# Recurrent block with FP4 side branch on one core: pointwise product and down product in fewer matmuls, down product moved ahead, GpSimd's sum moved, weight remainders made on TensorE

## The chip, the cores and the metric

The kernel runs on 1 core of one Trainium2 chip. The metric is device time in microseconds (us) of one execution. The engines are called by the profile's names: PE is TensorE, DVE is VectorE, ACT is ScalarE, POOL is GpSimd, SP is SyncE.

## What is computed

For x of 16 x 512 x 256 (batch, position, feature), with all products in float32 precision:

```python
xn = layernorm(x)
# branch s
a  = pointwise(causal_dwconv3(rmsnorm(xn, g0))) + b + xn       # 256 -> 256, over positions
hg = rmsnorm(a, g1) @ gru_w.T                                   # 256 -> 512, hidden and gate
h  = scan: h[t] = (1-sig(gate))*h[t-1] + sig(gate)*g(hidden)    # along the positions
b2 = h + a
s  = gelu(rmsnorm(b2, g2) @ w1.T + b1) @ w2.T + bias2 + b2      # 256 -> 1024 -> 256
# branch g, operands rounded to FP4 in blocks of 16 with a scale each
g  = silu( fp4(silu(fp4(xn) @ fp4(w_gate).T) * (fp4(xn) @ fp4(w_up).T)) @ fp4(w_down).T )   # 256 -> 704 -> 256
out = x + s * g
```

## The kernel before

**Tiling.** The program handles the batch in 16 chunks c = 0..15, each of L = 512 positions, as T = 4 token tiles of P = 128 (t); features are KD = 2 blocks of 128, the ff width is KF = 8 blocks, and the FP4 branch's 704 is KI = 6 blocks (NFULL = 5 full ones and a LAST of 64). Weights are loaded and prepared once, within chunk 0.

**Precision.** Except for the pointwise product, each operand is a pair of F32R tiles, a high part (`_hi`, an ACT copy) and a remainder (`_lo`, a DVE or POOL subtraction), and `product` (L982 to L991) issues three matmuls: hi.hi, hi.lo, lo.hi. `pointwise` (L1008) multiplies `pw` and `y` in float32. Transposes on PE are float32 matmuls against `ident`.

**Order.** There is no scheduler: each engine runs the program that is written out by hand, `first()`, then `body(c, front)` for c = 1..15, then `tail(15)`. Semaphores tie the engines. A body interleaves three chunks: gate_up, gru and ff1 of chunk c, the FP4 half behind `hid` and ff2 of chunk c-1, and the norm, FP4 rounding, convolution and pointwise of chunk c+1 (`front_...`).

**PE in a body** (L1239): gate_up(c,0,.), hq_transposes(c-1,1), gate_up(c,1,.), sum_squares, down(c-1,1), gate_up(c,2,.), spread_scale, hq_transposes(c-1,2), gate_up(c,3,.), down(c-1,2), gru(c), hq_transposes(c-1,3), ff2(c-1,0), ff2(c-1,1), sum_squares, down(c-1,3), spread_scale, ff2(c-1,3), ff2(c-1,2), ff1(c) with the transposes of `xc` in its middle, hq_transposes(c,0), transposes of `xq`, pointwise(c+1), down(c,0). One gate_up(c,t,u) is 12 matmuls of 352 columns, a `down` is 18 of 256, gru 24 of 512, ff2 for a tile 2 transposes and 24 of 256.

**What `down` waits for.** For each token tile: hidden (L496, DVE) multiplies `sl` (ACT) with the bank of gate_up; DVE rounds it to FP4 (L401 to L427, into `hq`); PE transposes `hq` (L1058); ACT copies the high part (`hqt_hi`, L812); DVE makes `hqt_lo` (L519, `hidden_low`); then `down` may start.

**The rms norms.** DVE adds the squares (`add_squares`, L524), PE transposes them (`sum_squares`), DVE sums and clamps (`clamp_sums`), POOL takes the power -1/2 (`inv_rms`, L348), PE spreads it (`spread_scale`), DVE scales (`scaled`, L539) and makes `xs_lo` (L545) beside ACT's `xs_hi`.

**POOL** also adds the residual for a whole chunk (`output_sum`, L356, 128 x 1024). Its wait `actlo_ready >= KF*(c+1)+5` lets it start when DVE has made five of the next chunk's eight `act_lo` tiles; two last chunks have no such wait. In chunk 0 POOL makes the remainders of the gru, w1 and w2 weights (`low_weights`, L363), while DVE and PE quantise and split the FP4 weights; PE fills gaps with small matmuls (`keep_busy`, L996).

## Time and profile before

| | us |
|---|---|
| three runs | 1084.11, 1086.87, 1087.17 |
| median | 1086.87 |
| the profiled execution | 1085.26 |
| its span, first to last instruction | 1083.5 |
| PE busy | 1061.8 (98%) |
| DVE busy | 934.5 (86%) |
| ACT busy | 607.3 (56%) |
| POOL busy | 147.5 (14%) |

The trace belongs to the profiled execution; 1.8 us of it lie outside the span. A row of the timeline has the start in us from the span's beginning, the length, engine, line, operation, output <- inputs, shapes and count, and, in brackets, how long the engine sat idle before it and what ended that. Neighbouring matmuls overlap in the rows, so the price of one is the distance between starts, not the length. Matmul ends are modelled.

### The profile page before, as it was taken

The page shows a single profiled execution, that of the slowest core. Times are in us where ns is not written, and L with a number is a line of the kernel's source. Part 1 is how long each engine was busy: PE and PEld are TensorE (multiplying, and loading weights), DVE is VectorE, ACT ScalarE, POOL GpSimd, SP SyncE. Part 2 cuts the span into 40 slices and gives each one's busy share as a digit, 9 for nine tenths or more (in the row PEclk, how much of TensorE's full clock was granted, in tenths as well). Part 3 has the DMA queues.
Part 4 walks back from the last instruction along what each step waited for, and adds up shares of the span by engine and source line. Part 5 has one row for each costly group of instructions (what it writes and reads, how often), then busy time and mean ns, then how long its engine had stood idle before and what let it go on. Part 6 is the DMA issues. An engine that isn't in the chain of part 4 may idle for free. (4 is left out here: it accounts for less than half of the span.)

```text
span 1083.5 us, 18319 instructions
## 1 busy us (share of the span) xinstructions
PE 1061.8 (98%) x6954; PEld 967.9 (89%) x6954; DVE 934.5 (86%) x1720; ACT 607.3 (56%) x967; POOL 147.5 (14%) x123
## 2 busy tenths in 40 slices
...
DMA packets 29365, 31.45 MB, mean 29 GB/s; under 512 B 1120, under 2 KB 28512, under 8 KB 29280
## 3 DMA queue, kind: packets, MB, share of 16 engines
...
## 5 line engine op out<-in xcount | busy, mean ns | idle before, releaser
L990 PE MATMUL gu_ps<-gu_hi,xq_hi 128*128 128x352 f32 x512 | 168.3, 329 | 0.0
L990 PE MATMUL gu_ps<-gu_lo,xq_hi 128*128 128x352 f32 x512 | 165.9, 324 | 0.0
L990 PE MATMUL gu_ps<-gu_hi,xq_lo 128*128 128x352 f32 x512 | 165.7, 324 | 0.0
L990 PE MATMUL w_ps<-w_hi,act_hi 128*128 128x256 f32 x480 | 140.1, 292 | 0.0
L990 PE MATMUL w_ps<-w_hi,act_lo 128*128 128x256 f32 x480 | 135.1, 281 | 0.0
L990 PE MATMUL w_ps<-w_lo,act_hi 128*128 128x256 f32 x480 | 134.9, 281 | 0.0
L990 PE MATMUL w_ps<-dn_hi,hqt_hi 128*128 128x256 f32 x384 | 116.6, 304 | 2.0 <-DVE hqt_lo L519 2.0
L990 PE MATMUL w_ps<-dn_hi,hqt_lo 128*128 128x256 f32 x384 | 108.5, 283 | 0.0
L990 PE MATMUL w_ps<-dn_lo,hqt_hi 128*128 128x256 f32 x384 | 108.4, 282 | 0.0
L818 ACT ACTIVATE g<-w_ps 128x256 f32<-128x256 f32 x64 | 24.7, 385 | 147.7 <-PE w_ps L990 147.6
L496 DVE TENSOR_TENSOR hid<-sl,gu_ps 128x704 f32<-128x704 f32 x64 | 56.8, 887 | 58.8 <-PE gu_ps L990 58.2
L990 PE MATMUL gu_ps<-xs_hi,w_hi 128*128 128x512 f32 x256 | 102.5, 400 | 0.4 <-DVE xs_lo L545 0.4
L990 PE MATMUL gu_ps<-xs_lo,w_hi 128*128 128x512 f32 x256 | 101.0, 395 | 0.0
L990 PE MATMUL gu_ps<-xs_hi,w_lo 128*128 128x512 f32 x256 | 101.0, 395 | 0.0
L990 PEld LDWEIGHTS gu_ps<-gu_hi,xq_hi 128*128 128x128 f32 x512 | 96.7, 189 | 0.2 <-issue 0.2
L990 PEld LDWEIGHTS gu_ps<-gu_lo,xq_hi 128*128 128x128 f32 x512 | 96.6, 189 | 0.0
L990 PEld LDWEIGHTS gu_ps<-gu_hi,xq_lo 128*128 128x128 f32 x512 | 96.3, 188 | 0.0
L842 ACT ACTIVATE act<-gu_ps,cols 128x512 f32<-128x512 f32 x128 | 86.1, 687 | 13.7 <-PE gu_ps L990 13.3
L812 ACT CAST hqt_hi<-w_ps 128x768 fp32r<-128x768 f32 x64 | 51.3, 802 | 73.0 <-PE w_ps L1058 72.2
L356 POOL TENSOR_TENSOR o<-o,x_res 128x1024 f32<-128x1024 f32 x15 | 36.1, 2403 | 400.8 <-issue 393.4
L990 PEld LDWEIGHTS w_ps<-w_lo,act_hi 128*128 128x128 f32 x480 | 90.6, 189 | 0.0
L990 PEld LDWEIGHTS w_ps<-w_hi,act_hi 128*128 128x128 f32 x480 | 90.4, 188 | 0.0
...
## 6 DMA issues: line engine op xcount, KB each, us to landing
...
```

The costliest lines, as they stand in the source:

```text
L356: nc.gpsimd.tensor_tensor(o[:], o[:], x_res[:], ALU.add).then_inc(out_ready, 1)
L496: V.tensor_tensor(hid[:, t, :].rearrange("p (h n) -> p h n", h=2), sl[:], gu_ps[:, 1, :, 0:HALF], ALU.mult).then_inc(hid_ready, 1)
L812: A.copy(hqt_hi[:], hqt_ps).then_inc(hqthi_ready, 1)
L818: A.activation(g[:, t, :], bank[:, 0:D], ACT.Silu).then_inc(g_ready, 1)
L842: A.activation(act1[:, j, :], ff1_bank(j), ACT.Gelu, bias=b1c[:, j:j + 1]).then_inc(gelu_ready, 1)
L990: done = M.matmul(psum, l, r, start=first and i == 0, stop=last and i == len(terms) - 1)
```

## The change

- **Pointwise.** `pw` and `y` become F32R pairs (`pw_hi`, `pw_lo`, `y_hi`, `y_lo`). A chunk's four float32 products become twelve F32R ones of 512 columns. ACT makes `y_hi` (2 copies a chunk), DVE `y_lo` (2 subtractions). All eight `xn` transposes stand ahead of the products.
- **Down.** `hq` now holds its last 64 columns twice (a second DVE instruction of 128 x 64), so the half-empty sixth block carries the high part in its lower and the remainder in its upper 64 rows of `hqt_hi`; `hidden_low` becomes two instructions. `down` has 17 matmuls instead of 18.
- **Order in a body, PE.** down(c-1,3) stands ahead of the squares' transposes; the `x2b` transposes of ff2 are split off (`ff2_open`); ff2(c-1,3) stands ahead of spread_scale, and the `xc` transposes ahead of ff2(c-1,2) and ff1.
- **Order in a body, DVE.** From chunk 2 on, bn_stats of chunk c+2 stands at the end of body c, and its aggregation (`front_moments`) in the next body behind hidden_values(c-1,2); the taps stand ahead of the rounding of `xq`; output(c-1,1) and `front_rows` are earlier. gelus_low is cut 4 + 4 instead of 5 + 3.
- **POOL.** The sum waits for 4 instead of 5 `act_lo` tiles, and in the two last chunks for all 8 (before: none). `low_weights` is gone.
- **Chunk 0.** The remainders of gru, w1 and w2 come from PE: ten pieces of 128 x 512, each a float32 matmul ident x source and an F32R one minus_ident x high part, copied by ACT (`weight_remainder`). DVE's and ACT's work in `first()` is re-ordered, and ff1 is interleaved with the FP4 weights; DVE's rounding of FP4 weight pieces 4 and 5 stands behind `scaled_low(1)`.
- **Last chunk.** In `tail`, ff2 of a tile stands ahead of its down, and DVE makes all `act_lo` before it rounds tile 2.
- **SP.** load(i+3) ahead of store(i).

```diff
 with sp.Fori(0, B - 3) as i:
+    load(i + 3)
     store(i)
-    load(i + 3)
 store(B - 3)
 store(B - 2)
 for t in range(T):
...
 def output_sum(c):
     pool.wait_ge(sg_ready, T * (c + 1))
-    if c < B - 2:
-        pool.wait_ge(actlo_ready, KF * (c + 1) + 5)
+    pool.wait_ge(actlo_ready, KF * (c + 1) + (4 if c < B - 2 else KF))
     pool.wait_ge(xres_ready, 16 * (c + 1))
     nc.gpsimd.tensor_tensor(o[:], o[:], x_res[:], ALU.add).then_inc(out_ready, 1)
...
-def front_moments(c):
+def fp4_hidden_values(dst, rounded):
+    n, last = NBI * FP4_BLOCK, NFULL * P // FP4_BLOCK
+    fp4_values(dst[:, 0:n], NBI, rounded)
+    return V.scalar_tensor_tensor(blocks(dst[:, n:KI * P], NBI - last),
+                                  blocks(q_m[:, NFULL * P:n].bitcast(BF16), NBI - last),
+                                  1.0 / UNIT, spread(q_scale[:, last:NBI], NBI - last),
+                                  ALU.mult, ALU.mult)
...
+def front_y_low(c):
+    for k in range(KD):
+        dve.wait_ge(yhi_ready, KD * c + k + 1)
+        V.tensor_tensor(y_lo[:, k, :], y[:, k, :], y_hi[:, k, :].bitcast(F32),
+                        ALU.subtract).then_inc(ylo_ready, 1)
...
-    fp4_values(hq[:, t % 2, 0:NI], NBI, rounded).then_inc(hq_ready, 1)
+    fp4_hidden_values(hq[:, t % 2, :], rounded).then_inc(hq_ready, 1)
...
     dve.wait_ge(hqthi_ready, T * c + t + 1)
     dve.wait_ge(dn_done, T * c + t)
-    V.tensor_tensor(hqt_lo[:], hqt_ps, hqt_hi[:].bitcast(F32), ALU.subtract).then_inc(hqtlo_ready, 1)
+    V.tensor_tensor(hqt_lo[:], hqt_ps[:, 0:NFULL, :], hqt_hi[:, 0:NFULL, :].bitcast(F32), ALU.subtract)
+    twin = hqt_hi[LAST:P, NFULL, :]
+    V.tensor_tensor(twin, hqt_ps[LAST:P, NFULL, :], twin.bitcast(F32),
+                    ALU.subtract).then_inc(hqtlo_ready, 1)
...
     hidden_values(c - 1, 1, fp4_round(NBI, carried["ratios"]))
-    gelus_low(c - 1, range(5))
+    gelus_low(c - 1, range(4))
     hidden(c, 0)
     scales = hidden_scales(c - 1, 2)
...
     clamp_sums(c * 2, w_ps[:, 0, :])
     hidden_values(c - 1, 2, fp4_round(NBI, ratios))
-    gelus_low(c - 1, range(5, KF))
+    if front and c > 1:
+        front_moments(carried["stats"])
+    gelus_low(c - 1, range(4, KF))
     hidden(c, 2)
     scaled(c * 2, x1, w_ps[:, 1, :], (x1_ready, KD * (c + 1)))
     scales = hidden_scales(c - 1, 3)
     dve.wait_ge(dve_step, ratios)
     hidden(c, 3)
     hidden_values(c - 1, 3, fp4_round(NBI, ratios))
-    if front:
-        front_moments(c + 1)
+    if front and c == 1:
+        front_moments(front_stats(c + 1))
     recurrence(c, 0)
     recurrence(c, 1)
     hidden_low(c - 1, 3)
...
         front_rows(c + 1)
+    clamp_sums(c * 2 + 1, gu_ps[:, 0, 0, :])
+    output(c - 1, 1, w_ps[:, 1, :])
     scales = hidden_scales(c, 0)
     scaled(c * 2 + 1, x1, gu_ps[:, 0, 1, :], (x2_ready, KD * (c + 1)))
     scaled_low(c * 2 + 1)
-    output(c - 1, 1, w_ps[:, 1, :])
     ratios = fp4_ratios(hid[:, 0, :], NBI, scales)
     hidden_values(c, 0, fp4_round(NBI, ratios))
     output(c - 1, 3, w_ps[:, 3, :])
     output(c - 1, 2, w_ps[:, 2, :])
     if front:
-        front_fp4_values(c + 1, front_fp4_ratios(c + 1))
+        ratios = front_fp4_ratios(c + 1)
         front_taps(c + 1)
+        front_fp4_values(c + 1, fp4_round(T * NBD, ratios))
+        front_y_low(c + 1)
         carried["ratios"] = fp4_ratios(hid[:, 1, :], NBI, hidden_scales(c, 1))
         hidden_low(c, 0)
         front_fp4_low(c + 1)
+        if c + 2 < B:
...
+def front_y_high(c):
+    for k in range(KD):
+        act.wait_ge(y_ready, KD * c + k + 1)
+        act.wait_ge(pw_done, KD * c)
+        act.wait_ge(x2_ready, KD * c)
+        A.copy(y_hi[:, k, :], y[:, k, :]).then_inc(yhi_ready, 1)
...
     high_part(c * 2 + 1, (hidden_done, KD * (c + 1)))
     biased_residual(c)
-    for j in range(KF // 2):
+    gelus(c, (0,))
+    if front:
+        front_y(c + 1)
+    gelus_high(c, (0,))
+    for j in range(1, KF // 2):
         gelus(c, (j,))
         gelus_high(c, (j,))
     if front:
-        front_y(c + 1)
-        gelus(c, range(KF // 2, KF))
+        gelus(c, range(KF // 2, KF - 2))
+        front_y_high(c + 1)
+        gelus(c, range(KF - 2, KF))
         hq_columns(c, 0)
         front_xq(c + 1)
...
 def pointwise(c):
+    pe.wait_ge(y_ready, KD * (c + 1))
     for e in range(KD):
-        pe.wait_ge(y_ready, KD * (c + 1))
         for t in range(T):
             M.matmul(w_ps[:, e, t * P:(t + 1) * P], xn[:, t, e * P:(e + 1) * P], ident[:],
                      is_transpose=True, start=t == 0, stop=False)
+    pe.wait_ge(yhi_ready, KD * (c + 1))
+    pe.wait_ge(ylo_ready, KD * (c + 1))
+    for e in range(KD):
         for k in range(KD):
-            last = product(w_ps[:, e, :], pw[:, k, e * P:(e + 1) * P], y[:, k, :], False, k == KD - 1)
+            last = product(w_ps[:, e, :], (pw_hi[:, k, e * P:(e + 1) * P], pw_lo[:, k, e * P:(e + 1) * P]),
+                           (y_hi[:, k, :], y_lo[:, k, :]), False, k == KD - 1)
         last.then_inc(pw_done, 1)
...
 def down(c, t, bank=w_ps[:, 2, :]):
     pe.wait_ge(hqthi_ready, T * c + t + 1)
     pe.wait_ge(hqtlo_ready, T * c + t + 1)
-    for k in range(KI):
-        last = product(bank[:, 0:D], (hqt_hi[:, k, :], hqt_lo[:, k, :]),
-                       (dn_hi[:, k, :], dn_lo[:, k, :]), k == 0, k == KI - 1)
-    last.then_inc(dn_done, 1)
+    for k in range(NFULL):
+        product(bank[:, 0:D], (hqt_hi[:, k, :], hqt_lo[:, k, :]), (dn_hi[:, k, :], dn_lo[:, k, :]),
+                k == 0, False)
+    M.matmul(bank[:, 0:D], hqt_hi[:, NFULL, :], dn_lo[:, NFULL, :], start=False, stop=False)
+    M.matmul(bank[:, 0:D], hqt_hi[:, NFULL, :], dn_hi[:, NFULL, :], start=False,
+             stop=True).then_inc(dn_done, 1)
...
+def ff2_open(c, t, bank, free):
+    pe.wait_ge(x2b_ready, KD * (c + 1))
+    pe.wait_ge(*free)
+    tok = slice(t * P, (t + 1) * P)
+    for k in range(KD):
+        M.matmul(bank[:, k * P:(k + 1) * P], x2b[:, k, tok], ident[:], is_transpose=True,
+                 start=k == 0, stop=False)
+def ff2(c, t, bank):
     pe.wait_ge(acthi_ready, KF * (c + 1))
     pe.wait_ge(actlo_ready, KF * (c + 1))
-    pe.wait_ge(x2b_ready, KD * (c + 1))
-    if free:
-        pe.wait_ge(*free)
     tok = slice(t * P, (t + 1) * P)
-    for k in range(KD):
...
+def remainder(i, free):
+    j, k, h = pieces[i]
+    cut = slice(h * L, (h + 1) * L)
+    pe.wait_ge(whi_ready, KD * j + k + 1)
+    pe.wait_ge(minus_ready, 1)
+    if free:
+        pe.wait_ge(*free)
+    M.matmul(piece_bank(i), ident[:], split_weights[j][1][:, k, cut], start=True, stop=False)
+    M.matmul(piece_bank(i), minus_ident, split_weights[j][2][:, k, cut], start=False,
+             stop=True).then_inc(rest_done, 1)
...
     gru(c, 1)
     hq_transposes(c - 1, 3, (g_ready, T * c - 1))
-    ff2(c - 1, 0, w_ps[:, 0, :], (ss_ready, 2 * c + 1))
-    ff2(c - 1, 1, w_ps[:, 1, :], (xs_ready, KD * (2 * c + 1)))
+    ff2_open(c - 1, 0, w_ps[:, 0, :], (ss_ready, 2 * c + 1))
+    ff2_open(c - 1, 1, w_ps[:, 1, :], (xs_ready, KD * (2 * c + 1)))
+    ff2(c - 1, 0, w_ps[:, 0, :])
+    ff2(c - 1, 1, w_ps[:, 1, :])
+    down(c - 1, 3)
     sum_squares(c * 2 + 1, gu_ps[:, 0, 0, :], (coef_ready, KD * c + 1))
-    down(c - 1, 3)
+    ff2_open(c - 1, 3, w_ps[:, 3, :], (hqtlo_ready, T * c))
+    ff2(c - 1, 3, w_ps[:, 3, :])
     spread_scale(c * 2 + 1, gu_ps[:, 0, 1, :], (cand_ready, KD * c + 1))
-    ff2(c - 1, 3, w_ps[:, 3, :], (hqtlo_ready, T * c))
-    ff2(c - 1, 2, w_ps[:, 2, :], (g_ready, T * c))
-    ff1(c, range(KF // 2))
     if front:
         pe.wait_ge(sg_ready, T * c - 2)
         front_xc(c + 1)
+    ff2_open(c - 1, 2, w_ps[:, 2, :], (g_ready, T * c))
+    ff2(c - 1, 2, w_ps[:, 2, :])
+    ff1(c, range(KF // 2))
+    if front:
         ff1(c, range(KF // 2, KF))
         hq_transposes(c, 0, (sg_ready, T * c))
...
+    down(c, 0, w_ps[:, 0, :])
+    hq_transposes(c, 1, (hqtlo_ready, T * c + 1))
+    last_open(0)
+    last_open(1)
+    last_ff2(0)
+    down(c, 1, w_ps[:, 1, :])
+    last_ff2(1)
+    for t in range(2, T):
+        hq_transposes(c, t, (hqtlo_ready, T * c + t))
+        last_open(t)
+        last_ff2(t)
+        pe.wait_ge(g_ready, T * c + t - 1)
         down(c, t, w_ps[:, t % 2, :])
-        if t < T - 1:
-            hq_transposes(c, t + 1, (hqtlo_ready, T * c + t + 1))
-        ff2(c, t, gu_ps[:, t // 2, t % 2, :], None)
 over_chunks(first, body)
```

What stands in a row at three places. **DVE in a body, from the second hidden product (L496 before, L511 now) to the third.** `hid` is the gated product, `hq` its FP4 values, `act_lo` the gelu remainders, `moments` the layernorm's. Before:

```order
L496 TENSOR_TENSOR hid<-sl,gu_ps 128x704
L413 SCALAR_TENSOR_TENSOR q_y<-hid,q_inv 128x704
L529 TENSOR_REDUCE ss_sum<-w_ps 128x4
L531 TENSOR_SCALAR ss_row<-ss_sum 128x4
L421 TENSOR_SCALAR q_e<-q_y 128x704
L423 TENSOR_SCALAR q_e<-q_e 128x704
L427 SCALAR_TENSOR_TENSOR hq<-q_e,q_scale 128x704
L512 TENSOR_TENSOR act_lo<-act,act_hi 128x512 x3
L496 TENSOR_TENSOR hid<-sl,gu_ps 128x704
```

and now:

```order
L548 TENSOR_REDUCE ss_sum<-w_ps 128x4
L550 TENSOR_SCALAR ss_row<-ss_sum 128x4
L419 TENSOR_SCALAR q_e<-q_y 128x704
L421 TENSOR_SCALAR q_e<-q_e 128x704
L425 SCALAR_TENSOR_TENSOR hq<-q_e,q_scale 128x704
L432 SCALAR_TENSOR_TENSOR hq<-q_e,q_scale 128x64
L447 MEMSET carrier 128x1
L449 BN_AGGR moments<-stats 128x2 x4
L453 TENSOR_SCALAR ln_in<-moments 128x4
L455 TENSOR_SCALAR rms_t<-moments 128x4
L527 TENSOR_TENSOR act_lo<-act,act_hi 128x512 x4
L511 TENSOR_TENSOR hid<-sl,gu_ps 128x704
```

The short duplicate, the aggregation and a fourth `act_lo` have come in between.

**PE in a body, around the second squares' transposes (`gu_ps<-ident,xs`).** `act` rows are ff2, `dn`/`hqt` rows are down(c-1,3). Before:

```order
L990 MATMUL w_ps<-w_lo,act_hi 128x256
L990 MATMUL w_ps<-w_hi,act_lo 128x256
L1042 MATMUL gu_ps<-ident,xs 128x128 x4
L990 MATMUL w_ps<-dn_hi,hqt_hi 128x256
L990 MATMUL w_ps<-dn_lo,hqt_hi 128x256
```

and now:

```order
L1063 MATMUL w_ps<-dn_hi,hqt_lo 128x256
L1146 MATMUL w_ps<-dn_lo,hqt_hi 128x256
L1147 MATMUL w_ps<-dn_hi,hqt_hi 128x256
L1119 MATMUL gu_ps<-ident,xs 128x128 x4
L1184 MATMUL w_ps<-ident,x2b 128x128 x2
L1063 MATMUL w_ps<-w_hi,act_hi 128x256
```

The down product has moved ahead of the transposes, ff2's tile 3 follows them, and the last two down rows are the merged sixth block.

**PE at the end of a body, the pointwise product.** `xn` is the residual that is transposed into the bank. Before:

```order
L1002 MATMUL gu_ps<-ident,xq 128x128 x8
L1013 MATMUL w_ps<-ident,xn 128x128 x4
L990 MATMUL w_ps<-cand,pw 128x512 x2
L1013 MATMUL w_ps<-ident,xn 128x128 x4
L990 MATMUL w_ps<-cand,pw 128x512 x2
L990 MATMUL w_ps<-dn_hi,hqt_hi 128x256
```

and now:

```order
L1075 MATMUL gu_ps<-ident,xq 128x128 x8
L1086 MATMUL w_ps<-ident,xn 128x128 x8
L1063 MATMUL w_ps<-y_hi,pw_hi 128x512
L1063 MATMUL w_ps<-y_lo,pw_hi 128x512
L1063 MATMUL w_ps<-y_hi,pw_lo 128x512
```

The transposes stand together, and the triple of F32R rows comes four times.

## Rows read from the trace of the kernel before

**Rows 1.** The page: busy time of each engine, share of the span, instructions.

```profile
PE 1061.8 (98%) x6954; PEld 967.9 (89%) x6954; DVE 934.5 (86%) x1720; ACT 607.3 (56%) x967; POOL 147.5 (14%) x123
```

**Rows 2.** Busy time by stretch; after the engines PEclk, DMA share, GB/s.

```profile
core 0: us, PE busy (x) PEld busy (x) DVE busy (x) ACT busy (x) POOL busy (x), PEclk, DMA share, GB/s
223.00:287.00 64.00, 63.79 (x418) 58.12 (x417) 56.04 (x104) 36.80 (x59) 8.77 (x7) 1.00 0.08 25
102.00:104.00 2.00, 2.00 (x11) 2.00 (x11) 1.83 (x4) 0.37 (x2) 0.00 (x0) 0.50 0.00 0
1058.00:1060.00 2.00, 0.29 (x3) 0.05 (x1) 2.00 (x5) 1.66 (x2) 0.00 (x0) 1.00 0.00 0
```

**Rows 3.** Chain that ended last: start, us, engine, output, line, matmuls.

```profile
994.01 1.72 PE w_ps L990 x4
...
1000.02 3.87 PE gu_ps L990 x24
...
1019.80 2.14 PE w_ps L990 x18
...
1021.94 5.57 PE gu_ps L990 x24
...
1058.29 1.74 issue
```

**Rows 4.** Timeline of PE: start of body 2, and the body from 488 us.

```profile
168.13 0.33 PE L990 MATMUL gu_ps<-gu_hi,xq_hi 128*128 128x352 f32 x1
...
488.03 0.33 PE L990 MATMUL gu_ps<-gu_hi,xq_hi 128*128 128x352 f32 x1
...
507.82 0.28 PE L990 MATMUL w_ps<-dn_hi,hqt_hi 128*128 128x256 f32 x1
...
525.39 0.65 PE L1050 MATMUL gu_ps<-ident,inv_rms 128*128 128x128 f32 x4 [0.22 <-POOL inv_rms L348]
```

**Rows 5.** Timeline of DVE in the same body.

```profile
492.18 0.89 DVE L496 TENSOR_TENSOR hid<-sl,gu_ps 128x704 f32<-128x704 f32 x1 [2.86 <-PE gu_ps L990]
...
496.69 0.89 DVE L496 TENSOR_TENSOR hid<-sl,gu_ps 128x704 f32<-128x704 f32 x1 [0.37 <-PE gu_ps L990]
...
503.13 0.89 DVE L496 TENSOR_TENSOR hid<-sl,gu_ps 128x704 f32<-128x704 f32 x1 [0.34 <-PE gu_ps L990]
...
506.61 0.89 DVE L519 TENSOR_TENSOR hqt_lo<-w_ps,hqt_hi 128x768 fp32r<-128x768 f32 x1
...
513.60 0.18 DVE L444 BATCH_NORM_AGGREGATE moments<-stats 128x2 f32<-128x6 f32 x1
...
514.16 0.68 DVE L551 SCALAR_TENSOR_TENSOR cand<-gu_ps,cand 128x512 f32<-128x512 f32 x1
...
526.82 1.22 DVE L539 TENSOR_TENSOR xs<-gu_ps,x 128x512 f32<-128x512 f32 x2
...
529.28 1.29 DVE L545 TENSOR_TENSOR xs_lo<-xs,xs_hi 128x512 fp32r<-128x512 f32 x2 [1.24 <-ACT xs_hi L799]
...
541.04 0.75 DVE L480 SCALAR_TENSOR_TENSOR cand<-w_ps,cols,cand 128x511 f32<-128x511 f32 x1 [1.01 <-ACT cand L756]
...
550.21 3.09 DVE L512 TENSOR_TENSOR act_lo<-act,act_hi 128x512 fp32r<-128x512 f32 x5
```

**Rows 6.** Timelines of POOL and DVE: residual sum, and DVE instructions beside POOL.

```profile
489.45 2.41 POOL L356 TENSOR_TENSOR o<-o,x_res 128x1024 f32<-128x1024 f32 x1 [28.10 <-issue]
...
1044.20 2.40 POOL L356 TENSOR_TENSOR o<-o,x_res 128x1024 f32<-128x1024 f32 x1 [7.38 <-DVE o L566]
...
1044.95 1.70 DVE L403 TENSOR_SCALAR q_wide<-q_amax 128x44 f32<-128x44 f32 x1
...
38.62 2.46 DVE L413 SCALAR_TENSOR_TENSOR q_y<-hid,q_inv 128x512 f32<-128x512 f32 x1
```

**Rows 7.** Timeline of PE at the end of chunk 0 and start of body 1.

```profile
100.41 0.36 PE L990 MATMUL w_ps<-dn_hi,hqt_hi 128*128 128x256 f32 x1 [1.97 <-DVE hqt_lo L519]
...
103.39 0.49 PE L990 MATMUL gu_ps<-gu_hi,xq_hi 128*128 128x352 f32 x1
```

More of the change, by code:

```diff
@@ L93, in mixed_recurrent_kernel @@
         ident = sb("ident", [P, P])
-        minus_ident = sb("minus_ident", [P, P], F32R)
         neg_half = sb("neg_half", [P, T])
@@ L101, in mixed_recurrent_kernel @@
         b1c = cols[:, KD * 9:KD * 9 + KF]
-        pw = sb("pw", [P, KD, D])
+        pw_hi = sb("pw_hi", [P, KD, D], F32R)
+        pw_lo = sb("pw_lo", [P, KD, D], F32R)
         gru_hi = sb("gru_hi", [P, KD, 2 * D], F32R)
@@ L137, in mixed_recurrent_kernel @@
         xs_lo = sb("xs_lo", [P, KD, L], F32R)
-        keep = sb("keep", [P, KD, L])
+        keep, y_hi = shared_home(("keep", [P, KD, L], F32), ("y_hi", [P, KD, L], F32R))
         take = xs
-        cand = sb("cand", [P, KD, L])
+        cand, y_lo = shared_home(("cand", [P, KD, L], F32), ("y_lo", [P, KD, L], F32R))
         y = cand
@@ L151, in mixed_recurrent_kernel @@
         hqt_hi = sb("hqt_hi", [P, KI, P], F32R)
-        hqt_lo = sb("hqt_lo", [P, KI, P], F32R)
+        hqt_lo = sb("hqt_lo", [P, NFULL, P], F32R)
         q_amax = sb("q_amax", [P, 64])
@@ L253, in mixed_recurrent_kernel, with piece_bank @@
                          (ld_w2, w2_f, halves(w2_hi), halves(w2_lo)))
+        pieces = [(j, k, h) for j, halved in ((0, 1), (1, 2), (2, 2)) for k in range(KD) for h in range(halved)]
+        def piece_bank(i):
+            return w_ps[:, 2 + i, :] if i < KD else w_ps[:, i % 2, :]
         def ff1_bank(j):
```

256 lines of the change are left out of this document (142 added, 114 removed).

## The prediction

> **What bounds the kernel now.** I read the page's busy shares first, then busy time by stretch, the chain that ended last, and the timelines of PE and DVE over one body. The shares name PE: 98% busy, DVE 86%, ACT 56% [rows 1]. By stretch, 64 us in the middle hold 63.79 us of PE and 56.04 us of DVE [rows 2]. Bodies 2 to 14 are alike: the first product of body 2 starts at 168.13 and that of body 15 at 1000.02 [rows 3, 4], so 13 periods of 63.99 us. In one period PE loses only about 0.4 us, before spread_scale, where it waits for POOL's inv_rms (0.22 us by the modelled ends, 0.42 us by the starts) [rows 4]. So PE's own work sets the period. The reader should see two things more: a matmul taken off PE counts in full only as long as DVE stays in time, and DVE has just 8 us of room in 64, spread over many small gaps.
>
> **Prices on PE.** By the chain, 4 instructions of the float32 pointwise take 1.72 us, so the 8 of a chunk (4 products, two instructions each) take 3.44; 24 F32R matmuls of 512 columns take 5.57, 0.232 each; a down of 18 takes 2.14, 0.119 each [rows 3].
>
> **The steady body, PE alone.** Pointwise: 12 x 0.232 = 2.79 instead of 3.44, -0.65. Down: four times one matmul, -0.48. The wait before spread_scale: today the squares' transposes are followed by one down (2.14) and then by 0.42 of waiting, so DVE's clamp and POOL's power need 2.56. In the new order ff2's tile 3 stands there, 24 x 0.119 + two transposes = 3.06, so the wait goes: -0.42, and -0.07 for a small gap ahead of the squares, which down(c-1,3) now covers. Splitting off ff2's transposes moves work and costs nothing, since consecutive starts add up either way. PE's own need falls by 1.62 to 62.37 us.
>
> **The steady body, what DVE adds.** Per chunk: y_lo, two subtractions at 0.60 from start to start, as act_lo of the same shape (five in 3.09 [rows 5]); four duplicates of 128 x 64, bounded by 0.07 (a twelfth of the 0.8 that hidden's 704 columns take) and 0.18 (the small aggregate at 513.60), I take 0.14; hidden_low in two instructions, +0.05 each. About 2 us, so 58 of 62.4. The question is where. Three places have to be followed.
>
> (a) *Tile 2's down.* hidden(c,1) starts when gate_up ends, at 496.69, and DVE's chain from there reaches the end of hqt_lo for down(c-1,2) at 506.61 + 0.89 = 507.50; PE starts that down at 507.82 [rows 4, 5]. Of these 10.81 us, 0.34 are a wait (at 503.13). Now the aggregation of the moments comes into this stretch (from 513.60 to 514.16 it takes 0.56), a fourth act_lo (0.60), a duplicate (0.14), the split (0.05): +1.35. It may use up the 0.34 wait and about 0.2 of the 0.32 margin, the rest being latency, and PE comes 0.12 earlier: PE waits about 0.9 us. hidden_low is needed there, so nothing hides it. From both sides: 0.6 if the duplicate and the split are nothing and the aggregation overlaps, 1.3 if each is twice as long.
>
> (b) *POOL's sum.* Today it starts at 489.45, just as DVE, done with five act_lo, waits for gate_up until 492.18, 2.86 us: nobody is hurt [rows 5, 6]. Where it does meet DVE, in the last body, it starts at 1044.20 and lasts 2.40 to 1046.60, and DVE's q_wide of 44 columns, issued at 1044.95, takes 1.70, where small instructions take 0.2 (0.18 at 513.60): it ends when POOL ends. Beside low_weights an instruction of 512 columns with two SBUF inputs takes 2.46, where that width takes 0.75 (541.04) [rows 5, 6]. Now the fourth act_lo frees the sum. When is that? DVE from scaled(2c+1) at 526.82 to the fifth act_lo at 550.21 + 3.09 = 553.30 takes 26.48, with waits of 1.24 and 1.01 [rows 5]. Without the waits, plus y_low (1.2, and 0.25 for ACT's y_hi), bn_stats (1.4), duplicates and split (0.3), 0.1 for xs_hi, less output(1) (0.33) and one act_lo (0.6): 26.6. PE from spread_scale (525.39) to the next gate_up (488.03 + 63.99) takes 26.6 now, 22.8 after the change (ff2's tile 3 is ahead of it, 3.06, and 0.65 + 0.12 go). DVE begins about 0.7 behind spread_scale's start, so the fourth act_lo ends 4.5 us into the next body, where today hidden(c,0) starts 4.15 in (492.18 against 488.03) [rows 4, 5]. The wait of 2.86 has been filled up, and POOL's sum runs from 4.6 to 7.0, beside hidden, the reduce and q_wide. Hidden and reduce go on, q_wide (due at 6.2) stands until 7.0. From there small instructions, the squares' sum and hidden_low take 2.2, so hqt_lo for down(c-1,1) ends 9.2 in, where PE wants it at 8.8 (two pairs of gate_up at 3.87 [rows 3], and transposes for 1.1): PE waits 0.5. Bounds: 0 (the sum finds a gap) to 1.5 (hidden itself is blocked).
>
> The Trainium skill bears on this, and against the change: its page "SBUF — State Buffer", section "Who interferes with whom", says that DVE and GpSimd share one port pair as an exclusive lock, that a tensor_scalar in a two-port mode or a DVE instruction with two SBUF inputs stands until GpSimd's instruction ends, and that an instruction with one SBUF input does not. By that rule q_wide waits and hidden (one input in PSUM) and the reduce pass, which gives 1076; without such a lock it would be 1069, the first rival. The trace's 1.70 and 2.46 agree with the rule.
>
> (c) *Tile 0's down and ff1.* y_hi, y_lo and the x transposes come about 1 us ahead of the pointwise, xs_lo 1 us ahead of ff1, hqt_lo of tile 0 0.3 us ahead of its down, by the same addition. No wait here, but little room: +0 to 0.5.
>
> A wait in (b) delays hidden(c,1) and so adds to (a). Together 1.4, and 0.1 for refilling PE: the period is 62.37 + 1.5 = 63.85, that is 0.14 less than now, 13 x 0.14 = **1.8 us**. Nearly all of the 1.62 a body that PE saves would turn into waits for DVE.
>
> **Chunk 0.** Today low_weights holds DVE up beside the w1 and the w2 remainders, each time a q_wide and a q_y, by about 1.7 us each (2.46 - 0.75) [rows 5, 6]; two idles of 2 us on PE (one of 1.97 is at 100.41) are each followed by a stretch at the lower clock (0.50 at 102 us) [rows 2, 7]. Against that, the pieces cost PE 10 x (0.86 + 0.23) = 10.9 us, but mostly in place of keep_busy matmuls, and pw_lo, which waits for pw's load, delays xn by about 1 us. Following DVE, ACT and PE through the new order, gru starts as now, the recurrence 3.4 us and ff1 4 us earlier (two of the four hold-ups are ahead of the recurrence), and the first gate_up of body 1 at 98 instead of 103.39 [rows 7]: **5.4 us** less, give or take 3. ACT, which makes ten more copies of 0.65 us, is what could cost most of this.
>
> **Body 1.** It takes 64.74 now, 0.75 over the period, through the low clock; that goes. It has no early aggregation, so (a) is 0.35 and (b) nearly nothing: **2.0 us** less.
>
> **Body 15 and tail.** The body saves as much as it waits. In the tail, PE idles 1.74 us for act_lo [rows 3]; that goes, as DVE makes them first, and the four shorter downs save 0.5; but the last product is now a down, behind which ACT's silu stands (about 0.5 us), and POOL's sum now falls into the tail (0.5): **1.5 us** less.
>
> **Sum.** 5.4 + 2.0 + 1.8 + 1.5 = 10.7. Span 1083.5 - 10.7 = 1072.8; with the 1.8 outside, 1074.6 for an execution that stood at 1085.26. The median of the runs stands 1.6 above that one: 1076.
>
> **Rivals.**
> *One wait only.* If (b) does not occur (the sum slips between), the period is 63.3, a further 13 x 0.55 = 7 us: 1069. For it: the bounds reach 0. Against it: DVE has no gap left there.
> *No new wait.* PE keeps its 62.37: 13 x 1.62 = 21 instead of 1.8: 1057. For it: PE is 98% busy and sets everything today. Against it: the addition in (a) rests on rows in the same places and needs an error of 0.9 us in 11.
> *The start gives nothing, or DVE is 0.5 us later a body:* 5.4 + 3 or 6.5 us are lost, 1083 to 1087: no change.
> *Slower: PE's clock falls at the new waits.* The wait in (a) is behind a full stretch and might be longer than I think. Behind the idle of 1.97 us at 100.41 the granted clock is 0.50, and the 18 matmuls to 103.39 take 2.98 instead of 2.14; with body 1's 0.75 that is 1.6 us for each fall [rows 2, 7]. Thirteen falls cost 21 us: 1097. It decides once a wait reaches about 2 us; an idle of 1.74 in the tail shows a clock of 1.00 [rows 2, 3], and I expect 0.9. The same price comes if hidden is blocked by the sum (1.5 a body).
>
> **How the numbers follow.** Forecast 1076 with 0.45, its own range 1070 to 1082; one wait 0.2; no wait 0.12; no change 0.1; slower 0.13. The range reaches from no new wait, 1057, to the forecast with the start 3 us and each body 0.7 us worse, 1088. A measurement of this kernel tells about 0.3% (3.3 us) from no change: faster 0.77, same 0.1, slower 0.13.
>
> **What would show it.** Right: a period of 63.7 to 64.0; PE idle for hqt_lo twice a body, at tile 1 (0.5) and tile 2 (1.0), and none before inv_rms; q_wide near 1 us long beside POOL's sum, itself 4.6 us into the body; body 1 starting near 98. Wrong: a period near 62.4 with no such waits, or PEclk under 1.00 in the middle.

## The result

| | before | after |
|---|---|---|
| median of the runs | 1086.86 | 1079.26 |
| the runs | 1084.11 to 1087.17 | 1078.19 to 1079.53 |
| the profiled execution | 1085.26 | 1078.19 |
| its span | 1083.5 | 1076.4 |

The changed kernel is 7.6 us faster, a ratio of 0.993 with a 95% interval of 0.991 to 0.995. I had forecast 1076.0, so the direction and nearly the size came true; of the 10.7 us that the sum promised, the span gave 7.1. In parts (starts of bodies 1, 2 and 15, and the end):

| stretch | before | after | gain | forecast |
|---|---|---|---|---|
| chunk 0 | 103.39 | 99.07 | 4.3 | 5.4 |
| body 1 | 64.74 | 63.10 | 1.6 | 2.0 |
| 13 bodies, each | 63.98 | 63.93 | 0.6 in all | 1.8 in all |
| body 15 and tail | 83.64 | 83.10 | 0.5 | 1.5 |

All starts are the first gate_up product of a body on PE's timeline: for before [rows 4, 7] and, for body 15,

```profile
999.86 0.32 PE L990 MATMUL gu_ps<-gu_hi,xq_hi 128*128 128x352 f32 x1
```

(the chain in [rows 3] has 1000.02, since it begins a piece where the matmul ahead of it ends), and for after

```profile
99.07 0.32 PE L1063 MATMUL gu_ps<-gu_hi,xq_hi 128*128 128x352 f32 x1
...
162.17 0.32 PE L1063 MATMUL gu_ps<-gu_hi,xq_hi 128*128 128x352 f32 x1
...
993.30 0.32 PE L1063 MATMUL gu_ps<-gu_hi,xq_hi 128*128 128x352 f32 x1
```

A period below is the mean of these 13 bodies; in the changed kernel a single body is up to 0.1 us off it.

The page of the changed kernel, busy time and share of each engine (before: [rows 1]):

```profile
PE 1046.4 (97%) x6914; PEld 969.0 (90%) x6914; DVE 978.1 (91%) x1883; ACT 626.5 (58%) x1010; POOL 124.2 (12%) x116
```

PE is busy 15.4 us less and the span is 7.1 shorter; DVE is busy 44 us more. The body that I had followed ([rows 4, 5]), now on PE (start, length, what; in brackets the idle time and what ended it); the rows are the body's start, down(c-1,1) and down(c-1,2):

```profile
481.87 0.32 PE L1063 MATMUL gu_ps<-gu_hi,xq_hi 128*128 128x352 f32 x1
...
491.15 0.36 PE L1063 MATMUL w_ps<-dn_hi,hqt_hi 128*128 128x256 f32 x1 [0.29 <-DVE hqt_hi L537]
...
503.05 0.36 PE L1063 MATMUL w_ps<-dn_hi,hqt_hi 128*128 128x256 f32 x1 [0.83 <-DVE hqt_hi L537]
```

and on DVE and POOL:

```profile
486.28 0.88 DVE L511 TENSOR_TENSOR hid<-sl,gu_ps 128x704 f32<-128x704 f32 x1
487.08 0.88 DVE L399 TENSOR_REDUCE q_amax<-hid 128x44 f32<-128x704 f32 x1
487.99 0.97 DVE L401 TENSOR_SCALAR q_wide<-q_amax 128x44 f32<-128x44 f32 x1
...
538.54 1.29 DVE L498 TENSOR_TENSOR y_lo<-cand,y_hi 128x512 fp32r<-128x512 f32 x2 [0.17 <-ACT y_hi L803]
```

```profile
486.50 2.42 POOL L367 TENSOR_TENSOR o<-o,x_res 128x1024 f32<-128x1024 f32 x1 [28.18 <-issue]
```

PE no longer waits for inv_rms; it waits twice a body for `hqt_lo` (whose second instruction writes `hqt_hi`), ahead of down(c-1,1) and down(c-1,2). POOL's sum starts 4.63 us into the body, and q_wide, small as it is, takes 0.97. Three rows of the waits, in the whole trace (engine and output that waited, who was waited for):

```profile
PE w_ps L1063 <- DVE hqt_hi L537: 16.7, 30, 1.1
...
DVE y_lo L498 <- ACT y_hi L803: 2.4, 13, 0.2
...
PE w_ps L1063 <- DVE y_lo L498: 0.8, 1, 0.8
```

The columns are us in total, times, the longest.

### The profile page after: what moved, and what is told of

It is laid out like the page before. It is cut to its first block, busy times and chain, and to the rows that moved or that the text cites. A ratio compares the mean times of both kernels' runs of the same rounds, so it can differ in the third digit from the quotient of the medians.

```text
span 1076.4 us, 18518 instructions
## 1 busy us (share of the span) xinstructions
PE 1046.4 (97%) x6914; PEld 969.0 (90%) x6914; DVE 978.1 (91%) x1883; ACT 626.5 (58%) x1010; POOL 124.2 (12%) x116
## 4 chain that ended last, share of the span: by engine, by line
PE 47%; DVE 36%; issue 8%; ACT 7%; ACTq 0%; DMA 0%; DVEq 0%
PE w_ps L1063 22%; PE gu_ps L1063 17%; DVE act_lo L527 5%; ACT act L888 4%; DVE hid L511 3%; DVE q_amax L399 3%; DVE hqt_lo L534 2%; DVE hq L425 2%; DVE xs L558 2%; DVE q_wide L401 2%; DVE xq_lo L504 2%; DVE y_lo L498 2%; DVE stats L441 2%; DVE q_y L411 1%; PE w_ps L1135 1%
## 5 line engine op out<-in xcount | busy, mean ns | idle before, releaser
L1063 PE MATMUL w_ps<-dn_hi,hqt_hi 128*128 128x256 f32 x320 | 92.9, 290 | 16.7 <-DVE hqt_hi L537 16.7
L1063 PEld LDWEIGHTS w_ps<-w_hi,act_lo 128*128 128x128 f32 x480 | 90.6, 189 | 0.0
L1063 PE MATMUL w_ps<-dn_hi,hqt_lo 128*128 128x256 f32 x320 | 90.3, 282 | 0.0
L1063 PE MATMUL w_ps<-dn_lo,hqt_hi 128*128 128x256 f32 x320 | 90.0, 281 | 0.0
L360 POOL TENSOR_TENSOR inv_rms<-ss_row,neg_half 128x4 f32<-128x4 f32 x32 | 35.9, 1120 | 456.6 <-DVE ss_row L550 456.6
```

Of the source, the lines that this page charges most:

```text
L360: nc.gpsimd.tensor_tensor(inv_rms[:], ss_row[:], neg_half[:], ALU.pow).then_inc(inv_ready, 1)
L1063: done = M.matmul(psum, l, r, start=first and i == 0, stop=last and i == len(terms) - 1)
```

## Experiments

Theory D, with which I went in: PE's saved time has become waits for DVE, in part because POOL's sum holds DVE. Rival P: PE's own matmuls still set the body, and its waits are incidental. Every run had the kernel before beside it on the same chip; ratios are to that, with their interval.

### Where DVE is late: the sum, the moments

**e1** frees the sum by a signal from DVE ahead of the taps, which read PSUM:

```diff
-pool.wait_ge(actlo_ready, KF * (c + 1) + (4 if c < B - 2 else KF))
+if c < B - 2:
+    pool.wait_ge(sum_go, c + 1)
+else:
+    pool.wait_ge(actlo_ready, KF * (c + 1) + KF)
...
 ratios = front_fp4_ratios(c + 1)
+V.memset(carrier[:], 0.0).then_inc(sum_go, 1)
 front_taps(c + 1)
```

> The changed kernel (1079.3 us, body 63.90), with POOL's residual sum released by a 1-column memset that DVE issues ahead of the convolution taps of the same body, instead of by the fourth act_lo of the next. The taps read one operand from PSUM. Theory D (the PE time saved has become waits for DVE, one of them through POOL's sum): q_wide falls from 0.97 to 0.19 us, the wait before down of tile 1 (0.3 to 0.45 us) goes, the one before tile 2 stays near 0.9, the taps keep 0.75 each; body 63.4 to 63.5, 1072 to 1074 us. Rival P (PE's own matmuls set the body, the waits are incidental and come back elsewhere): 1079, within 1.5.

**e2** puts `front_moments` back ahead of the recurrence, out of the chain (a) of the prediction:

```diff
 hidden_values(c - 1, 2, fp4_round(NBI, ratios))
-if front and c > 1:
-    front_moments(carried["stats"])
 gelus_low(c - 1, range(4, KF))
...
-if front and c == 1:
-    front_moments(front_stats(c + 1))
+if front:
+    front_moments(carried["stats"] if c > 1 else front_stats(c + 1))
```

> The changed kernel with one thing moved back: DVE's aggregation of the layernorm moments (0.56 us) stands behind hidden_values of tile 3, ahead of the recurrence, where DVE idles 0.86 us, instead of between the second and third hidden product. Theory D: the wait before down of tile 2 falls from 0.9 to about 0.35 us, nothing else grows, body 63.3 to 63.4, 1071 to 1073 us. Rival P: 1079, within 1.5.

**e4** does both, and moves the eighth act_lo behind hidden_values(c-1,3):

```diff
-gelus_low(c - 1, range(4, KF))
+gelus_low(c - 1, range(4, KF - 1))
...
 hidden_values(c - 1, 3, fp4_round(NBI, ratios))
+gelus_low(c - 1, (KF - 1,))
```

> The changed kernel with three moves on DVE and POOL and none on PE: the sum in the taps, the aggregation ahead of the recurrence, and the eighth act_lo there too (act_lo cut 4 + 3 + 1). Theory D: both waits go, PE's own 62.4 us set the body: 62.4 to 62.7, 1059 to 1064 us. If D is right on the two waits but the act_lo (0.6 us) only moves the wait to down of tile 3 or to the gelu of ff2: 62.9, 1066. Rival P: 1079, within 1.5.

Measured: e1 1071.65 (0.987, 0.985 to 0.989), e2 1070.58 (0.986, 0.984 to 0.988), e4 1058.79 (0.975, 0.973 to 0.978). All three by D, each at or just past the fast end of what I wrote; PE's matmuls are the same in them. The periods are 63.42, 63.37 and 62.45 us. No run has the first two moves alone, so what the moved act_lo adds in e4 is not known. In e1 the sum meets taps that read one input from PSUM, and they keep their 0.75:

```profile
529.99 2.41 POOL L371 TENSOR_TENSOR o<-o,x_res 128x1024 f32<-128x1024 f32 x1 [11.01 <-issue]
```

```profile
530.53 0.75 DVE L490 SCALAR_TENSOR_TENSOR cand<-w_ps,cols,cand 128x510 f32<-128x510 f32 x1
```

In e4 q_wide is back at 0.19, and PE's waits for `hqt_lo` are gone from bodies 2 to 15 (one is left in chunk 0, one in body 1 and the tail's of 1.1):

```profile
480.83 0.19 DVE L405 TENSOR_SCALAR q_wide<-q_amax 128x44 f32<-128x44 f32 x1
```

```profile
PE w_ps L1067 <- DVE hqt_hi L541: 2.0, 3, 1.1
```

From 474 to 500 us the chain that ended last runs through PE alone. Two body starts on it are 62.48 us apart; the mean from body 2 (162.49) to body 15 (974.39) is 62.45, and this is PE's own need in the changed order:

```profile
474.88 3.87 PE gu_ps L1067 x24
...
537.36 3.86 PE gu_ps L1067 x24
```

### What the single parts are worth

**e3** makes the pointwise product in float32 again (`pw` and `y` unsplit, no y_hi, no y_lo):

> The changed kernel with the pointwise product back in float32 (8 instructions of 0.43 us a chunk for 12 of 0.23; no y_hi, y_lo, pw_hi, pw_lo). PE has 0.65 us more a body, DVE 1.2 to 1.4 and ACT 1.2 less, ahead of the act_lo tiles. Theory D: POOL's sum starts 1.2 to 1.4 us earlier in the body and meets no q_wide, so the wait at tile 1 goes (0.45) and pays for most of PE's 0.65: body 63.9 to 64.1, 1079 to 1082 us. Rival P: each matmul counts in full, 15 x 0.65 = 10 more, 1089 us.

1080.07 (0.995, 0.993 to 0.997), against 1079.26: D. The period is 64.05, 0.12 more than in the changed kernel, though PE has 0.65 more to do: with y_lo gone PE no longer waits at tile 1 (0.53 by the starts), and 17 of its 30 waits are left:

```profile
PE w_ps L1052 <- DVE hqt_hi L536: 13.2, 17, 1.1
```

Within this order the part brought nothing, since its two y_lo came onto DVE. What it is worth beside e4's moves was not run.

**e9** makes `down` of 18 matmuls again, on the changed kernel; **e10** the same on e4:

```diff
-    fp4_values(dst[:, 0:n], NBI, rounded)
-    return V.scalar_tensor_tensor(blocks(dst[:, n:KI * P], NBI - last),
...
+    return fp4_values(dst[:, 0:NI], NBI, rounded)
...
-V.tensor_tensor(hqt_lo[:], hqt_ps[:, 0:NFULL, :], hqt_hi[:, 0:NFULL, :].bitcast(F32), ALU.subtract)
-twin = hqt_hi[LAST:P, NFULL, :]
...
+V.tensor_tensor(hqt_lo[:], hqt_ps, hqt_hi[:].bitcast(F32), ALU.subtract).then_inc(hqtlo_ready, 1)
...
-for k in range(NFULL):
...
+for k in range(KI):
```

> The changed kernel with the 18-matmul down again (no duplicate of the last 64 columns, one hidden_low instruction of 768 columns instead of two); all else stays. Theory D (in the changed kernel PE waits 1.45 us a body for DVE behind gate_up, so PE's matmuls there are not what sets the period; without the duplicate and the split DVE is 0.15 to 0.3 us a tile faster): the period changes by -0.2 to +0.2 us and the time is 1077 to 1082, with PE's waits for hqt_hi shrunk to under 10 us in sum. Rival P (PE's matmuls set the time): 64 downs x 0.119 = 7.6 us more, 1087.

> The version with room for DVE (the sum beside the taps, moments ahead of the recurrence, act_lo 4 + 3 + 1; 1058.8 us) with the 18-matmul down again. There PE waits for DVE only 2 us in all, so by theory D PE's matmuls now do set the time: 64 x 0.119 = 7.6 us more, 1065.5 to 1067, the period 62.9 to 63.0 instead of 62.50. Rival N (the merged down is worth little whatever DVE does, since its duplicate and split cost DVE as much as PE saves): 1058 to 1061.

e9: 1073.40 (0.988, 0.986 to 0.990), 5.9 us **faster** than the changed kernel, beyond both expectations; PE's waits for `hqt_lo` shrank to 7.0 us in 15, as expected, and the period to 63.55. e10: 1065.45 (0.980, 0.978 to 0.982), 6.7 us slower than e4, as expected, though not all of it by its price: the period grew by 0.41 a body, from 62.45 to 62.86, and body 1 began 1.8 later, with the clock at 0.87 from 50 to 60 us where e4 has 1.00. The same edit is worth 6 us one way or the other, by which engine sets the body. Its price on DVE is in the groups by line (busy time, mean ns of one) of the changed kernel,

```profile
L534 DVE TENSOR_TENSOR hqt_lo<-w_ps,hqt_hi 128x640 fp32r<-128x640 f32 x64 | 51.4, 803 | 2.6 <-ACT hqt_hi L858 2.4
L537 DVE TENSOR_TENSOR hqt_hi<-w_ps,hqt_hi 64x128 fp32r<-64x128 f32 x64 | 18.8, 295 | 0.9
L432 DVE SCALAR_TENSOR_TENSOR hq<-q_e,q_scale 128x64 f32<-128x64 bf16 x66 | 14.4, 218 | 0.0
```

and of e9:

```profile
L531 DVE TENSOR_TENSOR hqt_lo<-w_ps,hqt_hi 128x768 fp32r<-128x768 f32 x64 | 59.9, 936 | 3.9 <-ACT hqt_hi L852 3.9
```

The split costs 0.803 + 0.295 - 0.936 = 0.16 a tile and the duplicate 0.14 (495.25 to 495.39 from start to start), 0.30 together, against 0.05 to 0.13 on PE (the four downs of a body in e10 against e4, 0.41 in all). I had put the split at 0.05.

**e8** gives the weight remainders back to GpSimd (`low_weights` as before, small matmuls in the place of the pieces):

```diff
 def first():
     layernorm_scales(0, 1)
+    low_weights(0)
...
-remainder(2, (ss_ready, 1))
-remainder(3, (xs_ready, KD))
+keep_busy(8, gu_ps[:, 0, 0, :])
```

> The changed kernel, but the remainders of the gru, w1 and w2 weights are made by GpSimd again (six subtractions of 128 x 512 or 128 x 1024), with small filling matmuls on PE in place of the ten pieces and no copies of them on ACT. The rest of chunk 0's new order stays. Theory L (my forecast: GpSimd's subtractions hold DVE's instructions, each time by about 1.7 us, and that is what the pieces remove): two to four hold-ups come back, body 1 starts at 102 to 104 instead of 99.2, and the time is 1082 to 1084. Rival O (chunk 0 gained its 4 us by its new order, and the pieces on PE and ACT cost as much as GpSimd's lock did): body 1 starts at 98.5 to 100, 1078.5 to 1080.

1086.00 (1.000, 0.999 to 1.001): theory L, and more than it said. Body 1 starts at 105.64 instead of 99.07, so without the pieces the new order of chunk 0 would have lost 2.3 us against before. The reasons stand on POOL, DVE and PE:

```profile
51.25 5.12 POOL L373 TENSOR_TENSOR w_lo<-act,w_hi 128x1024 fp32r<-128x1024 f32 x2
...
76.14 5.39 POOL L373 TENSOR_TENSOR w_lo<-w_f,w_hi 128x1024 fp32r<-128x1024 f32 x2
```

```profile
53.40 3.51 DVE L576 TENSOR_TENSOR xs_lo<-xs,xs_hi 128x512 fp32r<-128x512 f32 x2
...
76.27 3.03 DVE L437 SCALAR_TENSOR_TENSOR hq<-q_e,q_scale 128x704 f32<-128x704 bf16 x1
79.22 2.39 DVE L444 SCALAR_TENSOR_TENSOR hq<-q_e,q_scale 128x64 f32<-128x64 bf16 x1
```

```profile
57.06 0.47 PE L1062 MATMUL gu_ps<-xs_hi,w_hi 128*128 128x512 f32 x1 [2.85 <-DVE xs_lo L576]
```

Two subtractions that take 1.29 elsewhere take 3.51 beside GpSimd, ff1 waits 2.85 for them, and the clock stands at 0.90 in the ten us from 60. Later `hq` takes 3.03 instead of 0.89 and the duplicate of 64 columns 2.39 instead of 0.22, and PE waits 1.27 (81.66) and 1.34 (83.88) behind them. What the ten pieces themselves cost PE and ACT was not measured apart.

**e6** lets POOL's sums of chunks 14 and 15 start without waiting for act_lo:

> The changed kernel, but GpSimd's residual sums of chunks 14 and 15 again start without waiting for the last act_lo, as in the kernel before; nothing else. The changed kernel's tail gave 0.5 us where I had forecast 1.5, and there q_wide (44 columns) takes 1.74 us beside the sum at 1052, behind which PE waits 1.11 us. Theory D (the sum holds DVE, and PE waits for that): the sum starts some 10 us sooner, beside DVE's work of body 15, q_wide in the tail takes 0.2, PE's wait of 1.11 falls to 0.5 or less, and the time is 0.5 to 1.0 us shorter: 1078.3 to 1078.8 beside a kernel before of 1086.9 (ratio 0.9920 to 0.9926). The sum may hold another DVE instruction instead, in body 15, by up to 1.5 us, where PE has about 0.5 us of room. Rival P (PE's own matmuls set the tail): no change, 1079.3, ratio 0.993.

1078.46 (0.993, 0.991 to 0.995): the median moved by 0.8, within what the runs scatter, so the time alone doesn't decide. The traces do for the mechanism. The changed kernel's tail on DVE and on PE:

```profile
1052.79 1.74 DVE L401 TENSOR_SCALAR q_wide<-q_amax 128x44 f32<-128x44 f32 x1
```

```profile
1056.30 0.36 PE L1063 MATMUL w_ps<-dn_hi,hqt_hi 128*128 128x256 f32 x1 [1.11 <-DVE hqt_hi L537]
```

and DVE in e6:

```profile
1041.00 1.70 DVE L402 TENSOR_SCALAR q_wide<-q_amax 128x44 f32<-128x44 f32 x1
...
1052.98 0.19 DVE L402 TENSOR_SCALAR q_wide<-q_amax 128x44 f32<-128x44 f32 x1
```

The hold-up moved to a place where nobody waits, and PE's wait of 1.11 went for one of 0.32 (at 1052.29, for act_lo). The span is 1.2 shorter, 1.1 of it behind the start of body 15 (993.23 in e6, 993.30 in the changed kernel).

### What closes the loop

Which stretch of DVE makes PE wait? I took the one from `scaled` (523.66) on, which has hardly a gap, and put PE's order around the squares back: in **e12** with DVE's order beside it, in **e13** the same on e4 (with e6's edit), in **e14** on PE alone.

```diff
-down(c - 1, 3)
 sum_squares(c * 2 + 1, gu_ps[:, 0, 0, :], (coef_ready, KD * c + 1))
+down(c - 1, 3)
+spread_scale(c * 2 + 1, gu_ps[:, 0, 1, :], (cand_ready, KD * c + 1))
 ff2_open(c - 1, 3, w_ps[:, 3, :], (hqtlo_ready, T * c))
 ff2(c - 1, 3, w_ps[:, 3, :])
-spread_scale(c * 2 + 1, gu_ps[:, 0, 1, :], (cand_ready, KD * c + 1))
```

> The changed kernel with one piece of its order undone: the squares' transposes stand ahead of down(c-1,3) again and spread_scale directly behind it, and DVE clamps ahead of front_rows and makes output(c-1,1) behind scaled_low, as in the kernel before. Theory D, in its sharper form: in the changed kernel DVE runs without a gap from scaled(2c+1) (523.66 in the trace) to hqt_lo for down(c-1,2) in the next body, and PE without a gap from that down (503.05) to spread_scale (523.66), so the period is the sum of these two stretches, 20.6 + 43.3. Undoing the order lets scaled begin about 4.43 us behind the squares' transposes at 517.51, at 521.9 instead of 523.66: the loop gets 1.7 shorter less 0.42 for the output that comes back into it, 62.6, and PE, with its wait of 0.42 back, needs 62.9. The period is 62.9 to 63.2 instead of 63.95, the time 1066 to 1071, though PE's own work gets no smaller and PE waits again before spread_scale. Rival P (PE's own work sets the period, and the removed wait is a gain): 14 x 0.42 = 6 us more, 1085.

> The version with room for DVE (the sum beside the taps, moments ahead of the recurrence, act_lo 4 + 3 + 1) and GpSimd's last sums sooner, with the squares' transposes ahead of down(c-1,3) again as in e12. Here PE does not wait for DVE, so by theory D the wait before spread_scale (0.42) now costs in full: period 62.9 instead of 62.50, 14 x 0.42 = 5.9 us more than e7, 1063 to 1065. If the squares' order were simply bad for another reason (its effect not hanging on DVE), it would be faster here too: under 1058.

> The changed kernel with PE's order alone undone: the squares' transposes ahead of down(c-1,3) and spread_scale directly behind it; DVE's and ACT's order stay as changed. (The run before this one that moved DVE's output(c-1,1) too got a wait of 1.9 us a body on PE, because the xc transposes need that output, and so did not tell the theories apart.) From the changed kernel's trace: squares at 517.51, front_rows on DVE until 518.99, clamp until 519.85, inv_rms until 520.95, so PE waits about 1.0 before spread_scale at 521.0, and scaled starts at 521.85 instead of 523.66. Loop account (theory D): DVE's stretch from scaled to down(c-1,2) of the next body starts 1.8 earlier, the loop shrinks to 62.1, and PE's own sum, 62.50 + 1.1 of wait, becomes what sets the period: 63.6 instead of 63.95, the waits for hqt_hi nearly vanish, and the time is 1074 to 1077. Rival P (waits for hqt_hi do not depend on when scaled starts, so the new wait before spread_scale is added): 14 x 1.1 = 15 us more, 1094.

Measured: e12 1122.2 (1.034, 1.032 to 1.035), e13 1098.23 (1.012, 1.011 to 1.014), e14 1096.40 (1.010, 1.008 to 1.012). My expectation failed in all three. In e12 and e13 the edit itself was bad: the xc transposes, which stand ahead of ff2(c-1,2) now, need output(c-1,1), which I had put behind scaled_low; they tell nothing of the theories but that. PE in e12:

```profile
541.50 1.09 PE L1075 MATMUL w_ps<-ident,xc 128*128 128x128 f32 x8 [1.85 <-DVE o L585]
```

e14 was clean, and it came out near the number of rival P (1094): the period grew by 1.10, to 65.03, which is the new wait, and the waits for `hqt_hi` stayed what they were, 16.5 us in 30 (16.7 in the changed kernel). PE, DVE and ACT in e14:

```profile
512.54 0.35 PE L1063 MATMUL w_ps<-dn_hi,hqt_hi 128*128 128x256 f32 x1 [0.82 <-DVE hqt_hi L537]
...
530.54 0.65 PE L1127 MATMUL gu_ps<-ident,inv_rms 128*128 128x128 f32 x4 [0.93 <-POOL inv_rms L360]
...
577.57 0.35 PE L1063 MATMUL w_ps<-dn_hi,hqt_hi 128*128 128x256 f32 x1 [0.82 <-DVE hqt_hi L537]
```

```profile
549.18 1.29 DVE L498 TENSOR_TENSOR y_lo<-cand,y_hi 128x512 fp32r<-128x512 f32 x2 [1.43 <-ACT y_hi L803]
```

```profile
538.24 1.34 ACT L880 ACTIVATE x2b<-x,cols 128x512 f32<-128x512 f32 x2 [5.06 <-PE w_ps L1063]
...
548.54 1.14 ACT L803 CAST y_hi<-cand 128x512 fp32r<-128x512 f32 x2
```

and ACT in the changed kernel:

```profile
527.60 1.34 ACT L880 ACTIVATE x2b<-x,cols 128x512 f32<-128x512 f32 x2 [2.00 <-PE w_ps L1063]
...
537.89 1.13 ACT L803 CAST y_hi<-cand 128x512 fp32r<-128x512 f32 x2
```

`scaled` did start sooner (18.69 behind down(c-1,2) instead of 20.61), but DVE then waited 1.13 for ff2's last product, 0.53 for the taps' input and 1.43 at y_lo, where the changed kernel has only 0.17 at y_lo. So the loop passes through three engines. From down(c-1,2) PE works without waiting for DVE to the end of ff2(c-1,2), which frees `x2b` for ACT to write again; ACT runs from x2b through the gelus, without a gap, to y_hi (1.28 of it is a load of the function table, at 529.04); DVE runs from y_lo without a gap to `hqt_lo` for down(c-1,2) of the next body. In the changed kernel: 527.60 - 503.05 = 24.55, 537.89 - 527.60 = 10.29, 0.65 to y_lo, and 28.4 to the next such down, 63.9. In e14: 25.70, 10.30, 0.64 and 28.39, 65.03. Only the first leg grew, by the new wait. The chain of the changed kernel that ended last shows the same path (start, length, engine, output):

```profile
527.56 1.40 PE gu_ps L1063 x6
...
530.34 0.69 ACT act L888
...
537.89 0.63 ACT y_hi L803
...
538.54 1.29 DVE y_lo L498 x2
...
566.50 0.30 DVE hqt_hi L537
...
566.94 1.07 PE w_ps L1063 x7
```

That it leaves PE at ff1's first tile and not at x2b is one link that I can't tell apart: both were there within 0.1 us. A version that moves x2b or y_hi on ACT was not tried, so the loop is read from the traces and from e14, and not proved by shortening ACT's leg.

Earlier runs fit it. e2 takes the moments (495.39 to 495.95, 0.56) out of DVE's leg, and the period falls by just that, 0.56. e9's DVE leg lacks two duplicates and three splits, 0.76, and its PE leg has 0.17 more for two downs: 0.59 less by the account, and 0.39 was measured, with DVE by then waiting 0.2 to 0.3 for gate_up ahead of two hidden products. e1 takes 0.78 of q_wide out, and the period falls by 0.51 only. There DVE waits for gate_up again ahead of hidden:

```profile
PE w_ps L1068 <- DVE hqt_hi L541: 13.2, 17, 1.1
...
DVE hid L515 <- PE gu_ps L1068: 4.6, 18, 0.9
```

So a second, shorter loop stands close behind the first: from the gate_up that hidden(c,1) waits for to down(c-1,2), which is the prediction's chain (a). In e1 and e3 it sets the one wait that is left, about 1.0 by the starts: 62.45 + 1.0 for e1, and 0.65 more for e3, against the measured 63.42 and 64.05.

### All that helped

**e7** is e4 with e6's edit.

> The version with room for DVE (e4: 1058.8 us) with GpSimd's residual sums of the two last chunks no longer waiting for act_lo. In the changed kernel alone that moved q_wide's hold-up from PE's path into body 15 and took 1.2 us off the span, 0.8 off the median. Theory D: 1057.5 to 1058.3. If nothing: 1058.8. It is the fastest version that I have.

1058.08 (0.974, 0.973 to 0.976), within what was expected: 28 us under the kernel before and 21 under the changed one, with PE busy in 99% of the span.

## Why the prediction was right, and where it was off

The forecast was 1076 and 1079.26 was measured, inside its own range of 1070 to 1082. Every part of the gain came out smaller than forecast, none larger.

*The waits: right.* Forecast 0.5 ahead of down(c-1,1) and 0.9 ahead of down(c-1,2), with 0.1 for refilling, 1.5 in all. Measured is 63.93 - 62.45 = 1.48, by the starts 0.5 and 1.0 at the two places named; the fourth act_lo ended 4.49 us into the body (forecast 4.5), the sum began at 4.63 (4.6), q_wide took 0.97 ("near 1"). e1, e2 and e4 show that DVE and the sum are the cause. By the rule of the Trainium skill ("SBUF — State Buffer", "Who interferes with whom") hidden and the reduce go on beside the sum, and q_wide waits. The trace agrees (0.88 and 0.88, against 0.97 where 0.19 is usual), and so do the taps of 0.75 in e1 and xs_lo of 3.51 in e8.

*What DVE starts from: wrong, and by luck without a price.* The prediction counted DVE's work in (b) from `scaled`, and took ACT's y_hi for a delay of 0.25 within it. e14 shows that y_hi is where DVE is tied: `scaled` started 1.9 us sooner and nothing behind y_lo did. In the changed kernel the two paths reach y_lo within 0.17 us of each other, so the 4.5 us came out right by either.

*PE's own need: mis-sized.* The term was 62.37, e4 shows 62.45. I took 0.119 for each dropped matmul, 0.48 for four; e10 against e4 gives 0.41, so 0.10 each. That is nearly all of the 0.08, and of a gain of 0.14 a body it left 0.05, 0.6 of 1.8 us in all. (62.37 + 1.5 is 63.87, which the prediction rounds to 63.85.)

*DVE's split: mis-sized too,* 0.16 instead of 0.05 a tile. The wait at tile 2 stayed within my bounds (0.6 to 1.3, by the starts 1.0). But it shows in e9: I had counted the merged down as a gain, and within this change it is a loss of 6 us. I had counted the pointwise part as a gain too, and within this change it is worth nothing clear of noise (e3). The prediction had priced the edits only as a sum, and the sum hid that.

*The wait ahead of spread_scale: right.* I gave its removal 0.49 a body, and it is gone from PE's waits. With 0.65 and 0.41 it makes 1.55, against the 1.53 by which e4's period lies under the one before. Putting PE's order back in the changed kernel costs more, 1.1 a body (e14), since there front_rows stands ahead of the clamp.

*Chunk 0: 4.3 for 5.4.* ff1 starts at 55.49 (forecast 4 us sooner than before's 59.13, so 55), and the recurrence 2.4 us sooner instead of 3.4. The rest was lost at its end, where PE waits 0.7 ahead of the xq transposes and 0.8 ahead of the products for y_lo of chunk 1, which I had not followed that far. e8 shows that taking the remainders off GpSimd is what made the new order pay; that this would be worth 6.6 us I did not foresee.

*Body 1: 1.6 for 2.0.* It takes 63.10, where 62.74 was forecast. Its one wait for `hqt_lo`, 0.30 at tile 2, is near the 0.35 of the forecast, so the rest is PE's other time in this body, and I have not followed it further.

*Body 15 and tail: 0.5 for 1.5.* I charged the sum in the tail with 0.5. It cost PE a wait of 1.11 (q_wide takes 1.74), and e6 gives back 1.1 there. The silu behind the last down cost 0.35 (0.45 from the last product's end to DVE's next instruction, where it was 0.10), less than the 0.5 that I took.

*The rivals.* "No new wait" (1057) is what e4 reached, 1058.8: the bound was sound, for a kernel that moves three things more. The rival of no change adds up to 1082.5 or 1084.4 by its own terms, not to 1087. A fall of the clock was not put to the test by the changed kernel: PEclk is 1.00 in its bodies, and no wait of PE in them is above 0.84. e12 comes nearest. PE waits about 1.9 ahead of the xc transposes in each of its bodies (26.2 us in 14); two of its seven executions show a mean clock of 1.000 and took 1114.9 and 1115.2 us, the other five show 0.988 to 0.994 and took 1122.0 to 1128.4. The kept trace is of one of the two, so where the clock fell in the others, and behind which wait, is not shown.
